# A gated cross-attention kernel: VectorE's softmax stage written as one list, with ScalarE's context copies and VectorE's Newton roots removed

## The chip, the cores and the metric

The kernel runs on one core of one Trainium2 chip. The metric is the device time of one execution in microseconds (us).

## What is computed

For each of 8 batches, `x` is 512 x 512 and the memory is 1601 x 256, all float32:

```python
memory_proj = einsum('bme,de->bmd', memory, W_mem)
scores = einsum('bnd,bmd->bnm', x, memory_proj) / sqrt(D)
attn = softmax(scores, axis=-1)
memory_context = einsum('bnm,bmd->bnd', attn, memory_proj)
gate = sigmoid(einsum('bnf,df->bnd', concatenate([x, memory_context], -1), W_gate) + b_gate)
fused = x + gate * memory_context
out = fused * rsqrt(mean(square(fused), -1) + 1e-6) * norm_w
```

## The kernel before, in words

The projection is never formed. The kernel multiplies x by `W_mem` (q, 256 columns), takes scores of q against the raw memory, sums the raw memory weighted by the exponentials (u), and only then multiplies u by `W_mem` (context) and by `V`, the product of `W_mem` and the second half of `W_gate` (gate). Each float32 factor is split into a rounded part (`_hi`, written by ScalarE) and the rest (`_lo`, written by VectorE, line 838), and each product takes three matmuls: hi by hi, hi by lo, lo by hi (lines 357 to 359, and 524 to 526 for the weighted sum).

The program is written by hand, one list for each engine, with semaphores between them. Each list has a repeat for b = 0, a hardware loop for b = 1 to 6, a repeat for b = 7 and a tail. One repeat has two stages.

**Scores stage.** TensorE computes 13 tiles of scores (the last of 65 rows). ScalarE copies each to `s` (`copy_s`), VectorE keeps a running maximum (L850) and splits the memory (`mem_lo`, pairs 0 to 5 of tiles here, by the table `SPLIT_BY_SCORES`).

**Softmax stage.** TensorE goes through this list: row sums of batch b - 1 (L459), its gate and context products for its four row tiles j, the x part of the gate of batch b for j = 0 to 3 (`gate_x`), then 13 tiles of the weighted sum, t = 0 to 12. Behind t = 9 stands the query product of batch b + 1 (`QUERY_AT = 9`). `gate_x` alternates between two PSUM banks, so from j = 2 it waits until VectorE's `add_bias` (L905) of j - 2 has emptied the bank; the query waits until VectorE's fourth `xt_lo` part, the rest of x transposed for batch b + 1, is written:

```python
pe.wait_ge(gx_done, NT * b + j - 1)
pe.wait_ge(xt_has_lo, DT * (b + 2))
```

Meanwhile, for each t, VectorE subtracts the column maximum (`shift`, L879), ScalarE takes the exponential (L673) and rounds it (L635), VectorE writes the rest (`p_lo_part`), and GpSimd adds the exponential to the row sums (`add_p`, L1155, 12 adds in a repeat). The epilogue of batch b - 1 is spread through VectorE's list by tables and conditions on t: `gate_input` (L934), `gate_ctx` (L984), `add_x` (L991); ScalarE does the `tanh`, scales the context out of PSUM by half the reciprocal row sum (`copy_ctx`, L696) and sums squares (L710). Then VectorE computes the reciprocal root by a bit trick and three Newton steps (`rms`, 11 small operations) and scales four tiles (`output`, L1020), which SyncE stores. The transposes of x and of the memory for batch b + 1 (L944, L960) stand in the same list.

In the tail, after b = 7, VectorE multiplies by `norm_w` ahead of the root (L1017) and ScalarE scales two of the four tiles (L831).

Of the kernel before, what the change touches and what calls it, by code (L numbers as in the profile page):

```python
# [30 lines left out]
ALU = mybir.AluOpType  # L31
# [6 lines left out]
P = 128  # L38
# [4 lines left out]
RSQRT_MAGIC = float(0x5F3759DF)  # L43
NEWTON_STEPS = 3


def xattn_kernel(nc: bass.Bass, x, mem, w, wg, b_gate, norm_w, out):
# [17 lines left out]
    with ExitStack() as ctx:  # L65
# [58 lines left out]
        nw_a = sb("nw_a", [P, NT])  # L124
        nw_b = sb("nw_b", [P, NT])
# [51 lines left out]
        ctx_copied, tanh_done, squares_done = sem("ctx_copied"), sem("tanh_done"), sem("squares_done")  # L177
# [7 lines left out]
        newton, out_done = sem("newton"), sem("out_done")  # L185

        normed, tail_done = sem("normed"), sem("tail_done")

        p_added = sem("p_added")

        NEWTON_OPS = 2 + 3 * NEWTON_STEPS
# [8 lines left out]
        X_AT = [6, 7, 9, 10]  # L200

        X_BLOCKS_AT = [4, 5, 7, 8]
        MEM_BLOCKS_AT = [10, 11]

# [30 lines left out]
        def _(sp):  # L235
# [103 lines left out]
            for j in range(NT):  # L339

                if 0 < j < NT - 1:
                    sp.wait_ge(tail_done, j)
                else:
                    sp.wait_ge(out_done, NT * (B - 1) + (1 if j == 0 else 2))
                sp.dma_start(out[B - 1, j * P : (j + 1) * P, :], fused[:, j, :]).then_inc(fused_free[j], 16)
# [6 lines left out]
        def _(pe):  # L352
# [280 lines left out]
        def _(act):  # L633
# [55 lines left out]
            def copy_ctx(b, j):  # L689

                act.wait_ge(pe_ctx, NT * b + j + 1)
                if j == 0:
                    act.wait_ge(r_done, b + 1)

                act.wait_ge(fused_free[j], 16 * (b + 1))
                nc.scalar.activation(fused[:, j, :], bank[CTX_BANK + j % 2][:, :], ACT.Copy,  # L696
                                     scale=r_half[:, j : j + 1]).then_inc(ctx_copied, 1)

# [51 lines left out]
            def iteration(b, first, last):  # L750
# [11 lines left out]
                if first:  # L762
                    for g in [*WG1T, V[0]]:
                        weights(g)
                    for t in range(MT + 1):
                        for q in SPLIT_BY_SOFTMAX.get(t, []):
                            mem_hi_part(b, q, first)
                        softmax(b, t, first)
                        if t == 1:
                            weights(V[1])  # L770
                        if not last and t - 1 in X_AT:
                            xt_hi_part(b + 1, X_AT.index(t - 1), False)
                        if not last and t == 12:
                            q_hi_part(b + 1, 0)
                            q_hi_part(b + 1, 1)
                else:
                    tanh(b - 1, 0)
                    copy_ctx(b - 1, 0)
                    tanh(b - 1, 1)
                    for t in range(MT + 1):  # L780
                        for q in SPLIT_BY_SOFTMAX.get(t, []):
                            mem_hi_part(b, q, first)
                        softmax(b, t, first)
                        if t in (0, 2, 3):
                            copy_ctx(b - 1, max(t, 1))
                        if t in (2, 3):
                            tanh(b - 1, t)
                        if t == 1:
                            squares(b - 1, 0)
                        if t - 2 in ADD_AT:  # L790
                            squares(b - 1, ADD_AT.index(t - 2) + 1)
                        if not last and t - 1 in X_AT:
                            xt_hi_part(b + 1, X_AT.index(t - 1), False)
                        if not last and t == 13:
                            q_hi_part(b + 1, 0)
                            q_hi_part(b + 1, 1)
# [23 lines left out]
            for j in range(NT):  # L820
                tanh(B - 1, j)
                copy_ctx(B - 1, j)
                if j >= 1:
                    squares(B - 1, j - 1)
            squares(B - 1, NT - 1)

            act.wait_ge(normed, NT - 1)

            act.wait_ge(newton, NEWTON_OPS * B)
            for j in range(1, NT - 1):  # L830
                nc.scalar.activation(fused[:, j, :], gate[:, j, :], ACT.Copy,  # L831
                                     scale=r_rms[:, j : j + 1]).then_inc(tail_done, 1)
# [3 lines left out]
        def _(dve):  # L836
# [54 lines left out]
            def softmax(b, t, with_x):  # L891

                if t + 3 < MT:
                    shift(b, t + 3)
                if with_x and t in X_AT:
                    xt_lo_part(b + 1, X_AT.index(t))
                p_lo_part(b, t)

# [38 lines left out]
            def transpose_x(b, k):  # L937

                if k >= 2:

                    dve.wait_ge(xt_has_lo, DT * b + k - 1)

# [4 lines left out]
            def transpose_mem(b, p):  # L947


                if p < 2:  # L950
                    dve.wait_ge(in_blocks[0], 16 * CT * BLOCKS * b)
                    if p == 1:
# [11 lines left out]
            def transpose_next(b, t, first):  # L964
                if t in X_BLOCKS_AT:
                    if t == X_BLOCKS_AT[0]:
                        if first:

                            dve.wait_ge(wt_split_lo, 8)
                        else:  # L970

                            dve.wait_ge(ctx_copied, NT * b)
                    transpose_x(b + 1, X_BLOCKS_AT.index(t))
                if t in MEM_BLOCKS_AT:
                    if t == MEM_BLOCKS_AT[0] and not first:

                        dve.wait_ge(z_done, NT * b)
                    transpose_mem(b + 1, MEM_BLOCKS_AT.index(t))
# [8 lines left out]
            def add_x(b, j):  # L987

                dve.wait_ge(gated, NT * b + j + 1)
# [4 lines left out]
            def rms(b):  # L994

                count = [NEWTON_OPS * b]

                def link(instruction):

                    count[0] = count[0] + 1  # L1000
                    instruction.then_inc(newton, 1)
                    dve.wait_ge(newton, count[0])


                dve.wait_ge(squares_done, NT * (b + 1))
# [186 lines left out]
```

## Time and profile before

| | |
|---|---|
| median of 3 runs | 561.4 us (561.13 to 561.5) |
| the profiled execution | 562.44 us, its span 560.6 us |
| busy: TensorE, VectorE | 541.7 us (97%), 503.4 us (90%) |
| busy: ScalarE, GpSimd | 336.2 us (60%), 134.1 us (24%) |
| one repeat, from one row sum to the next (b = 4) | 66.0 us |
| TensorE's mean granted clock | 0.99 |

Engines in the rows: PE is TensorE, PEld its weight loads, DVE VectorE, ACT ScalarE, POOL GpSimd. A duration in a row is longer than the engine's pitch: the next instruction starts before the last one's writes are seen. The pitch is read from the starts of neighbouring rows. Times of a timeline are counted from the start of the span.

### The profile page before, as it was taken

To read this page: it belongs to the slowest core of one execution; us is meant where nothing else is said; L and a number is where in the kernel's file an instruction comes from. 1 tells how busy PE (TensorE), PEld (TensorE's weight loads), DVE (VectorE), ACT (ScalarE), POOL (GpSimd) and SP (SyncE) were. 2 spreads that over 40 slices of the span, in tenths; PEclk is the share of its full clock that TensorE was granted. 3 is DMA by queue.
4 is the path that set the end of the run, shared out by engine and by line. 5 is a ranking of instruction groups with operands and counts; after the bars stand their busy time and mean duration, and the time that the engine had idled before them with its cause. 6 is when DMAs were issued, how large, how long until landed. Compare 5 with 4: busy or idle time off the path is not lost.

```text
span 560.6 us, 9004 instructions
## 1 busy us (share of the span) xinstructions
PE 541.7 (97%) x2432; PEld 438.8 (78%) x2432; DVE 503.4 (90%) x847; ACT 336.2 (60%) x633; POOL 134.1 (24%) x102
## 2 busy tenths in 40 slices
PE   8999999999999999999999999999999999999992
PEld 7777888878887788878888788887888778887871
DVE  4879959999899998899998998999988999889966
ACT  4676646665567646576366665666565864667534
POOL 0005600244003520055001440025300451005600
PEclk9999999999999999999999999999999999999988
DMA  9965371520683117711385115841088212100033
GB/s 226 260 127 83 90 132 50 98 73 18 148 176 97 37 50 136 167 68 37 98 163 104 56 37 134 171 114 40 0 170 177 75 37 99 52 23 20 0 114 112
DMA packets 184338, 54.25 MB, mean 97 GB/s; under 512 B 161528, under 2 KB 174848, under 8 KB 184320
## 3 DMA queue, kind: packets, MB, share of 16 engines
q1 hardware_dynamic: 183792, 53.52, 40.9%
q10 hardware_dynamic: 528, 0.52, 0.3%
q8 instruction: 8, 0.13, 0.1%
q14 instruction: 10, 0.08, 0.0%
HBM read 45.63 MB, written 8.39 MB: 96 GB/s over the span
## 4 chain that ended last, share of the span: by engine, by line
PE 66%; DVE 17%; issue 10%; SPq 3%; ACT 2%; DMA 2%; ACTq 0%; DVEq 0%
PE bank L357 14%; PE bank L358 13%; PE bank L359 13%; PE bank L524 7%; PE bank L525 7%; PE bank L526 7%; DVE p_lo L838 5%; DVE s L879 3%; DVE fused L984 2%; DVE fused L991 2%; DVE gate L905 2%; ACT fused L696 2%; DVE gate L934 2%; DMA fused<-in_L_xattn_W_gate_dram 2%; SPq L249 2%
## 5 line engine op out<-in xcount | busy, mean ns | idle before, releaser
L1155 POOL TENSOR_TENSOR psum_rows<-psum_rows,p_tmp 128x512 f32<-128x512 f32 (+1 forms) x88 | 122.5, 1392 | 85.4 <-ACT p_tmp L673 84.3
L838 DVE TENSOR_TENSOR p_lo<-p_tmp,p_hi 128x512 fp32r<-128x512 f32 (+1 forms) x104 | 92.3, 889 | 5.5 <-ACT p_hi L635 5.4
L673 ACT ACTIVATE p_tmp<-s 128x512 f32<-128x512 f32 (+1 forms) x104 | 65.2, 628 | 45.1 <-DVE s L879 44.5
L1155 POOL TENSOR_TENSOR psum_rows<-p_tmp 128x512 f32<-128x512 f32 x8 | 10.8, 1354 | 309.4 <-ACT p_tmp L673 309.4
L357 PE MATMUL bank<-q_hi,mt_hi 128*128 128x512 f32 (+1 forms) x208 | 81.7, 393 | 0.0
L358 PE MATMUL bank<-q_lo,mt_hi 128*128 128x512 f32 (+1 forms) x208 | 81.2, 390 | 0.0
L359 PE MATMUL bank<-q_hi,mt_lo 128*128 128x512 f32 (+1 forms) x208 | 81.1, 390 | 0.0
L525 PE MATMUL bank<-p_lo,mem_hi 128*128 128x512 f32 (+1 forms) x208 | 81.0, 389 | 0.0
L524 PE MATMUL bank<-p_hi,mem_hi 128*128 128x512 f32 (+1 forms) x208 | 81.0, 389 | 0.0
L526 PE MATMUL bank<-p_hi,mem_lo 128*128 128x512 f32 (+1 forms) x208 | 80.9, 389 | 0.0
L635 ACT ACTIVATE s<-bank 128x512 f32<-128x512 f32 (+1 forms) x104 | 62.0, 597 | 19.5 <-PE bank L359 19.1
L879 DVE TENSOR_TENSOR s<-s,bank 128x512 f32<-128x512 f32 (+1 forms) x104 | 68.5, 672 | 0.0
L850 DVE TENSOR_TENSOR run<-run,s 128x512 f32<-128x512 f32 (+1 forms) x88 | 59.9, 680 | 8.0 <-ACT s L635 5.6
L635 ACT ACTIVATE p_hi<-p_tmp 128x512 fp32r<-128x512 f32 (+1 forms) x104 | 63.5, 617 | 0.0
L357 PE MATMUL bank<-wg1t_hi,xt_hi 128*128 128x512 f32 x128 | 51.9, 405 | 5.9 <-DVE gate L905 5.9
L358 PE MATMUL bank<-wg1t_lo,xt_hi 128*128 128x512 f32 x128 | 49.9, 390 | 0.0
L359 PE MATMUL bank<-wg1t_hi,xt_lo 128*128 128x512 f32 x128 | 49.9, 390 | 0.0
L635 ACT ACTIVATE mt_hi<-bank 128x512 fp32r<-128x512 f32 (+1 forms) x56 | 30.2, 554 | 28.9 <-PE bank L359 28.9
L838 DVE TENSOR_TENSOR mt_lo<-bank,mt_hi 128x512 fp32r<-128x512 f32 (+1 forms) x56 | 34.5, 625 | 12.4 <-ACT mt_hi L635 12.4
L526 PEld LDWEIGHTS bank<-p_hi,mem_lo 128*128 128x128 f32 (+1 forms) x208 | 39.0, 188 | 8.2
L702 ACT ACTIVATE gate<-gate 128x512 f32<-128x512 f32 x32 | 20.2, 633 | 42.0 <-DVE gate L934 42.0
L524 PEld LDWEIGHTS bank<-p_hi,mem_hi 128*128 128x128 f32 (+1 forms) x208 | 39.0, 188 | 8.2
(93 smaller groups left out, 1057.6 us busy)
## 6 DMA issues: line engine op xcount, KB each, us to landing
mem_raw<-in_ctx_dram SPq DMA_DIRECT2D x48, 256.0 KB, 3.0
mem_blocks<-in_ctx_dram SPq DMA_DIRECT2D x64, 136.0 KB
x_again<-in_x_dram SPq DMA_DIRECT2D x32, 256.0 KB, 2.6
out_dram<-fused SPq DMA_DIRECT2D x32, 256.0 KB, 2.1
x_raw<-in_x_dram SPq DMA_DIRECT2D x112, 64.0 KB, 2.1
mem_blocks<-in_ctx_dram SPq DMA_DIRECT2D x56, 64.0 KB, 2.0
x_raw<-in_x_dram SPq DMA_DIRECT2D x4, 256.0 KB, 4.7
gate<-in_L_xattn_W_gate_dram SPq DMA_DIRECT2D x2, 512.0 KB, 6.1
```

The source lines that it names most:

```text
L357: nc.tensor.matmul(dst, a_hi, b_hi, start=(start and i == 0), stop=False)
L358: nc.tensor.matmul(dst, a_hi, b_lo, start=False, stop=False)
L359: last = nc.tensor.matmul(dst, a_lo, b_hi, start=False, stop=(stop and i == n - 1))
L524: nc.tensor.matmul(dst, mem_hi[0:r, t, cs], p_hi[0:r, t, :], start=(t == 0), stop=False)
L525: nc.tensor.matmul(dst, mem_hi[0:r, t, cs], p_lo[0:r, t % LO_RING, :], start=False, stop=False)
L526: last = nc.tensor.matmul(dst, mem_lo[0:r, t, cs], p_hi[0:r, t, :], start=False, stop=(t == MT - 1))
L635: return nc.scalar.activation(dst, src, ACT.Copy)
L673: nc.scalar.activation(p_tmp[0:r, t % TMP_RING, :], s[0:r, t, :], ACT.Exp, scale=float(D) ** -0.5).then_inc(exp_done, 1)
L838: return nc.vector.tensor_tensor(dst, src, hi.bitcast(F32), ALU.subtract)
L850: nc.vector.tensor_tensor(run[0:r, :], a, s[0:r, t, :], ALU.max).then_inc(run_done, 1)
L879: nc.vector.tensor_tensor(s[0:r, t, :], s[0:r, t, :], bank[MAX_BANK][0:r, :], ALU.subtract).then_inc(shifted, 1)
L1155: nc.gpsimd.tensor_tensor(psum_rows[0:r, :], a, p_tmp[0:r, t % TMP_RING, :], ALU.add).then_inc(p_added, 1)
```

## The change

1. `gate_ctx` reads the context from its accumulator bank in PSUM and no longer waits for a copy; ScalarE's `copy_ctx` is gone. The factor `r_half` moves into `add_x`, which becomes a scalar_tensor_tensor with a scalar per partition. TensorE's third and fourth context products now wait for `gated` in place of `ctx_copied`.
2. In the loop the root moves from VectorE to GpSimd: two small operations and a power with exponent -0.5, on 128 x 4 elements, behind its add for t = 9. VectorE's 11 Newton operations are gone; it waits for `rms_done` before the four outputs.
3. VectorE's softmax stage is one straight list, the same for all repeats but for the parts of the first and the last. Three of the epilogue's operations come earlier, the splits of memory pairs 4 and 5 move here from the scores stage, and the `xt_lo` parts stand behind `p_lo` of t = 8, 9, 10 and 11, in place of 5, 6, 8 and 9.
4. ScalarE's list follows: `tanh` behind t = 0, 2 (as 1, 2, 3 for j = 1, 2, 3), squares behind t = 3, 4, 5, 7, the hi parts of memory pairs 4 to 6 behind t = 6, 7, 8, the hi parts of x behind t = 9 to 12.
5. The tail computes the root in two parts, of tiles 0 to 2 and of tile 3: VectorE the mean, GpSimd the power, and VectorE all four outputs.

```diff
-        X_AT = [6, 7, 9, 10]
-        X_BLOCKS_AT = [4, 5, 7, 8]
-        MEM_BLOCKS_AT = [10, 11]
-        ADD_AT = [1, 3, 11]
-        SPLIT_BY_SCORES = {0: [0], 2: [1], 4: [2], 5: [3], 6: [4, 5]}
-        SPLIT_BY_SOFTMAX = {5: [6]}
+        SPLIT_BY_SCORES = {0: [0], 2: [1], 4: [2], 5: [3]}
+        SPLIT_BY_SOFTMAX = {6: 4, 7: 5, 8: 6}
+        TANH_AT, SQUARES_AT, NEXT_X_AT = {0: 1, 2: 2, 3: 3}, {3: 0, 4: 1, 5: 2, 7: 3}, {9: 0, 10: 1, 11: 2, 12: 3}
+        RMS_AT = 9
...
-                    pe.wait_ge(ctx_copied, NT * b + j - 1)
+                    pe.wait_ge(gated, NT * b + j - 1)
...
                 dve.wait_ge(tanh_done, NT * b + j + 1)
-                dve.wait_ge(ctx_copied, NT * b + j + 1)
-                nc.vector.scalar_tensor_tensor(fused[:, j, :], gate[:, j, :], 1.0, fused[:, j, :],
+                dve.wait_ge(pe_ctx, NT * b + j + 1)
+                dve.wait_ge(fused_free[j], 16 * (b + 1))
+                nc.vector.scalar_tensor_tensor(fused[:, j, :], gate[:, j, :], 1.0, bank[CTX_BANK + j % 2][:, :],
                                                ALU.add, ALU.mult).then_inc(gated, 1)
...
-                nc.vector.tensor_tensor(fused[:, j, :], fused[:, j, :], x_again[:, j % 2, :],
-                                        ALU.add).then_inc(fused_done, 1)
+                nc.vector.scalar_tensor_tensor(fused[:, j, :], fused[:, j, :], r_half[:, j : j + 1],
+                                               x_again[:, j % 2, :], ALU.mult, ALU.add).then_inc(fused_done, 1)
...
+                    gate_ctx(b - 1, 1)
+                    gate_input(b - 1, 2)
+                    add_x(b - 1, 1)
+                shift(b, 3)
+                p_lo_part(b, 0)
...
+                shift(b, 5)
+                p_lo_part(b, 2)
+                if not first:
+                    add_x(b - 1, 3)
+                add_bias(b, 0, first)
+                shift(b, 6)
+                p_lo_part(b, 3)
+                if not last:
+                    transpose_x(b + 1, 0, first)
+                shift(b, 7)
+                add_bias(b, 1, first)
...
+            def rms(b):
+
+                pool.wait_ge(squares_done, NT * (b + 1))
+                nc.gpsimd.tensor_tensor(mean_sq[:, :], sq_sum[:, :], one_in_d[:, :], ALU.mult).then_inc(mean_done, 1)
+                pool.wait_ge(mean_done, b + 1)
+                nc.gpsimd.tensor_tensor(mean_sq[:, :], mean_sq[:, :], eps_rows[:, :], ALU.add).then_inc(guarded, 1)
+                pool.wait_ge(guarded, b + 1)
+                nc.gpsimd.tensor_tensor(r_rms[:, :], mean_sq[:, :], minus_half[:, :], ALU.pow).then_inc(rms_done, 1)
...
+            gate_input(B - 1, 0)
             for j in range(NT):
+                gate_ctx(B - 1, j)
+                add_x(B - 1, j)
+                if j + 1 < NT:
+                    gate_input(B - 1, j + 1)
+                if j == NT - 2:
+                    tail_mean_sq(slice(0, NT - 1))
+
+            dve.wait_ge(rms_done, B)
+            output(B - 1, 0)
+            tail_mean_sq(slice(NT - 1, NT))
+            output(B - 1, 1)
+            output(B - 1, 2)
+
+            dve.wait_ge(rms_done, B + 1)
+            output(B - 1, 3)
```

Where the list moves VectorE's work, first place: the hardware loop, up to the first `add_bias` (gate<-bank,bias_rows), for which TensorE's third `gate_x` waits. Before:

```order
L934 SCALAR_TENSOR_TENSOR gate<-bank,r_sum,gate 128x512
L991 TENSOR_TENSOR fused<-fused,x_again 128x512
L879 TENSOR_TENSOR s<-s,bank 128x512
L838 TENSOR_TENSOR p_lo<-p_tmp,p_hi 128x512
...
L934 SCALAR_TENSOR_TENSOR gate<-bank,r_sum,gate 128x512
L984 SCALAR_TENSOR_TENSOR fused<-gate,fused 128x512
L879 TENSOR_TENSOR s<-s,bank 128x512
L838 TENSOR_TENSOR p_lo<-p_tmp,p_hi 128x512
...
L905 TENSOR_TENSOR gate<-bank,bias_rows 128x512
```

and in the change:

```order
L923 SCALAR_TENSOR_TENSOR fused<-gate,bank 128x512
...
L878 SCALAR_TENSOR_TENSOR gate<-bank,r_sum,gate 128x512
...
L933 SCALAR_TENSOR_TENSOR fused<-fused,r_half,x_again 128x512
L831 TENSOR_TENSOR s<-s,bank 128x512
L790 TENSOR_TENSOR p_lo<-p_tmp,p_hi 128x512
L923 SCALAR_TENSOR_TENSOR fused<-gate,bank 128x512
L831 TENSOR_TENSOR s<-s,bank 128x512
L790 TENSOR_TENSOR p_lo<-p_tmp,p_hi 128x512
L933 SCALAR_TENSOR_TENSOR fused<-fused,r_half,x_again 128x512
...
L849 TENSOR_TENSOR gate<-bank,bias_rows 128x512
```

The additions of x for tiles 2 and 3 (fused<-fused,r_half,x_again) and the gate product of tile 3 (fused<-gate,bank) now stand ahead of this `add_bias`, where three of them stood behind it.

Second place: the same loop, up to the fourth `xt_lo`, for which TensorE's query product waits. Before:

```order
L838 TENSOR_TENSOR p_lo<-p_tmp,p_hi 128x512
L944 STREAM_TRANSPOSE bank<-x_raw 128x512
L879 TENSOR_TENSOR s<-s,bank 65x512
...
L838 TENSOR_TENSOR xt_lo<-bank,xt_hi 128x512
L838 TENSOR_TENSOR p_lo<-p_tmp,p_hi 128x512
...
L838 TENSOR_TENSOR xt_lo<-bank,xt_hi 128x512
L838 TENSOR_TENSOR p_lo<-p_tmp,p_hi 128x512
...
L960 STREAM_TRANSPOSE bank<-mem_blocks 128x512
L991 TENSOR_TENSOR fused<-fused,x_again 128x512
L838 TENSOR_TENSOR p_lo<-p_tmp,p_hi 128x512
L960 STREAM_TRANSPOSE bank<-mem_blocks 128x512
L838 TENSOR_TENSOR p_lo<-p_tmp,p_hi 65x512
```

and in the change:

```order
L790 TENSOR_TENSOR p_lo<-p_tmp,p_hi 128x512
L790 TENSOR_TENSOR mem_lo<-mem_raw,mem_hi 65x256
...
L790 TENSOR_TENSOR xt_lo<-bank,xt_hi 128x512
L894 STREAM_TRANSPOSE bank<-x_raw 128x512
L790 TENSOR_TENSOR p_lo<-p_tmp,p_hi 128x512
...
L790 TENSOR_TENSOR xt_lo<-bank,xt_hi 128x512
...
L914 STREAM_TRANSPOSE bank<-mem_blocks 128x512
L790 TENSOR_TENSOR p_lo<-p_tmp,p_hi 128x512
...
L790 TENSOR_TENSOR xt_lo<-bank,xt_hi 128x512
L914 STREAM_TRANSPOSE bank<-mem_blocks 128x512
L790 TENSOR_TENSOR p_lo<-p_tmp,p_hi 65x512
```

The fourth `xt_lo` stood ahead of `p_lo` of t = 10 and of both transposes of the memory; now `p_lo` of t = 10 and 11 and the first of these transposes stand ahead of it.

## Rows read from the trace of the kernel before

**Rows 1.** Page, part 1: busy us (share of span) and instructions of each engine.

```profile
PE 541.7 (97%) x2432; PEld 438.8 (78%) x2432; DVE 503.4 (90%) x847; ACT 336.2 (60%) x633; POOL 134.1 (24%) x102
```

**Rows 2.** Waits, all engines: engine, line waited for: us in total, times, longest us.

```profile
PEld bank L357 <- DVE gate L905: 11.9, 14, 1.1
...
DVE fused L984 <- ACT fused L696: 7.1, 14, 0.8
```

**Rows 3.** Timeline of PE, repeat b = 4: start us, us, engine, line, op, names, shapes, count.

```profile
295.50 0.95 PE L459 MATMUL bank<-ones,psum_rows 128*128 128x1 f32 x8
...
313.44 0.39 PE L359 MATMUL bank<-wg1t_hi,xt_lo 128*128 128x512 f32 x1
...
314.02 0.50 PE L357 MATMUL bank<-wg1t_hi,xt_hi 128*128 128x512 f32 x1 [0.19 <-DVE gate L905]
...
316.65 0.39 PE L359 MATMUL bank<-wg1t_hi,xt_lo 128*128 128x512 f32 x1
...
317.73 0.50 PE L357 MATMUL bank<-wg1t_hi,xt_hi 128*128 128x512 f32 x1 [0.69 <-DVE gate L905]
...
334.18 0.39 PE L357 MATMUL bank<-xt_hi,w_hi 128*128 128x512 f32 x1
...
361.50 0.95 PE L459 MATMUL bank<-ones,psum_rows 128*128 128x1 f32 x8
```

**Rows 4.** Timeline of DVE, repeat b = 4, around the waits.

```profile
298.55 0.75 DVE L934 SCALAR_TENSOR_TENSOR gate<-bank,r_sum,gate 128x512 f32<-128x512 f32 x1
...
301.28 0.74 DVE L934 SCALAR_TENSOR_TENSOR gate<-bank,r_sum,gate 128x512 f32<-128x512 f32 x1
...
302.54 1.88 DVE L879 TENSOR_TENSOR s<-s,bank 128x512 f32<-128x512 f32 x3
...
313.29 0.68 DVE L905 TENSOR_TENSOR gate<-bank,bias_rows 128x512 f32<-128x512 f32 x1
...
331.95 0.67 DVE L838 TENSOR_TENSOR xt_lo<-bank,xt_hi 128x512 fp32r<-128x512 f32 x1
```

**Rows 5.** Timeline of DVE and POOL, repeat b = 4: work that shares SBUF reads.

```profile
305.87 1.19 DVE L838 TENSOR_TENSOR p_lo<-p_tmp,p_hi 128x512 fp32r<-128x512 f32 x1
...
309.29 1.62 DVE L838 TENSOR_TENSOR p_lo<-p_tmp,p_hi 128x512 fp32r<-128x512 f32 x1
...
317.60 1.15 DVE L984 SCALAR_TENSOR_TENSOR fused<-gate,fused 128x512 f32<-128x512 f32 x1
...
305.15 1.36 POOL L1155 TENSOR_TENSOR psum_rows<-p_tmp 128x512 f32<-128x512 f32 x1 [37.97 <-ACT p_tmp L673]
```

**Rows 6.** Timeline of DVE, end of the stage: the roots and the four outputs.

```profile
336.67 0.14 DVE L1006 TENSOR_SCALAR mean_sq<-sq_sum 128x4 f32<-128x4 f32 x1
...
338.82 2.74 DVE L1020 SCALAR_TENSOR_TENSOR fused<-fused,r_rms,norm_rows 128x512 f32<-128x512 f32 x4
```

**Rows 7.** Timeline of ACT and POOL, repeat b = 4: an exponential and the add it feeds.

```profile
306.10 0.62 ACT L673 ACTIVATE p_tmp<-s 128x512 f32<-128x512 f32 x1
...
306.89 1.33 POOL L1155 TENSOR_TENSOR psum_rows<-psum_rows,p_tmp 128x512 f32<-128x512 f32 x1 [0.38 <-ACT p_tmp L673]
```

**Rows 8.** Groups by line: us busy, mean ns of one | idle before, releaser.

```profile
L1155 POOL TENSOR_TENSOR psum_rows<-psum_rows,p_tmp 128x512 f32<-128x512 f32 (+1 forms) x88 | 122.5, 1392 | 85.4 <-ACT p_tmp L673 84.3
...
L1180 POOL MEMSET const-float32-1.0<- 128x1 f32 x1 | 0.1, 99 | 0.0
```

**Rows 9.** Timeline of PE and DVE, first repeat, b = 0.

```profile
49.36 0.67 DVE L905 TENSOR_TENSOR gate<-bank,bias_rows 128x512 f32<-128x512 f32 x1
...
70.12 0.39 PE L357 MATMUL bank<-xt_hi,w_hi 128*128 128x512 f32 x1
```

**Rows 10.** Timeline of DVE, tail after the last repeat.

```profile
539.77 0.75 DVE L934 SCALAR_TENSOR_TENSOR gate<-bank,r_sum,gate 128x512 f32<-128x512 f32 x1 [1.41 <-PE bank L359]
...
555.95 0.75 DVE L1020 SCALAR_TENSOR_TENSOR fused<-fused,r_rms,norm_rows 128x512 f32<-128x512 f32 x1
```

**Rows 11.** Page, part 6: DMA issues, KB each, median us to landing.

```profile
out_dram<-fused SPq DMA_DIRECT2D x32, 256.0 KB, 2.1
```

More of the change, by code:

```diff
@@ L339, in _ @@
             for j in range(NT):
[L341 to L345, printed above, removed]
+                store(B - 1, j)
             for j in range(NT):
@@ L687, in softmax @@
                     p_hi_part(b, t - 1)
[L689 to L697, printed above, removed]
             def tanh(b, j):
@@ L764, in iteration @@
                         weights(g)
[L765 to L775, printed above, removed]
                 else:
                     tanh(b - 1, 0)
[L778 to L796, printed above, removed]
+                for t in range(MT + 1):
+                    softmax(b, t, first)
+                    if first and t == 1:
+                        weights(V[1])
+                    if not first and t in TANH_AT:
+                        tanh(b - 1, TANH_AT[t])
+                    if not first and t in SQUARES_AT:
+                        squares(b - 1, SQUARES_AT[t])
+                    if t in SPLIT_BY_SOFTMAX:
+                        mem_hi_part(b, SPLIT_BY_SOFTMAX[t], first)
+                    if not last and t in NEXT_X_AT:
+                        xt_hi_part(b + 1, NEXT_X_AT[t], False)
+                if not last:
+                    q_hi_part(b + 1, 0)
+                    q_hi_part(b + 1, 1)
                 if not last:
@@ L821, in _ @@
                 tanh(B - 1, j)
[L822 to L832, printed above, removed]
+                squares(B - 1, j)
         @block.vector
@@ L962, in transpose_mem @@
                     mem_blocks[:, :, r0:r1, :]).then_inc(mt_done, 1)
[L964 to L978, printed above, removed]
@@ L1055, in iteration @@
                     shift(b, 2)
-                    for t in range(MT):
-                        for q in SPLIT_BY_SOFTMAX.get(t, []):
-                            mem_lo_part(b, q)
-                        softmax(b, t, not last)
-                        if t == 1:
-                            weights(V[1])
-                        if 1 <= t < 1 + NT:
-                            add_bias(b, t - 1, first)
-                        transpose_next(b, t, first)
                 else:
@@ L1090, in iteration @@
-                    rms(b - 1)
+                    gate_ctx(b - 1, 1)
[3 more added lines that the diff above has]
+                p_lo_part(b, 0)
+                if first:
+                    weights(V[1])
+                else:
+                    gate_ctx(b - 1, 2)
+                    gate_input(b - 1, 3)
+                    add_x(b - 1, 2)
+                shift(b, 4)
+                p_lo_part(b, 1)
+                if not first:
+                    gate_ctx(b - 1, 3)
@@ new lines, in iteration @@
+                p_lo_part(b, 5)
+                add_bias(b, 2, first)
+                shift(b, 9)
+                p_lo_part(b, 6)
+                mem_lo_part(b, 4)
+                shift(b, 10)
+                add_bias(b, 3, first)
+                p_lo_part(b, 7)
+                mem_lo_part(b, 5)
+                shift(b, 11)
+                p_lo_part(b, 8)
+                if not last:
+                    xt_lo_part(b + 1, 0)
+                    transpose_x(b + 1, 2, first)
+                shift(b, 12)
@@ new lines, in iteration @@
+                p_lo_part(b, 9)
+                mem_lo_part(b, 6)
+                if not last:
+                    xt_lo_part(b + 1, 1)
+                    transpose_x(b + 1, 3, first)
+                p_lo_part(b, 10)
+                if not last:
+                    xt_lo_part(b + 1, 2)
+                    transpose_mem(b + 1, 0, first)
+                p_lo_part(b, 11)
+                if not last:
+                    xt_lo_part(b + 1, 3)
+                    transpose_mem(b + 1, 1, first)
@@ L1091, in iteration @@
+                p_lo_part(b, 12)
+                if not first:
+                    dve.wait_ge(rms_done, b)
                     for j in range(NT):
```

98 lines of the change are left out of this document (38 added, 60 removed).

## Prediction

> **What bounds the kernel now.** I read the page's busy shares first, then the waits, then the timeline of one repeat in the loop. TensorE is busy for 541.7 us of the 560.6 [rows 1], so at most 19 us of gaps can be won, and every new gap on it is paid in full. Its waits inside the repeats have one name: `add_bias`, whose 14 waits come before the third and fourth `gate_x` [rows 2]. In repeat b = 4 the second `gate_x` issues its last matmul at 313.44, the next could follow 0.23 us later at 313.67 and starts at 314.02 (0.35 late); the fourth could start at 316.88 and starts at 317.73 (0.85 late) [rows 3]. So a repeat of 66.0 us has 1.2 us of waiting. The query product at 334.18 follows without a wait. VectorE is what TensorE waits for: from 301.28 on it works through its list with hardly a break, and its first `add_bias` starts at 313.29 [rows 4]. Each place of that list therefore has a due time: the two `add_bias` are late already, and the fourth `xt_lo`, from 331.95 to 332.62, is 1.5 us early for the query [rows 3, 4].
>
> **Prices.** VectorE's pitch for 128 x 512 is 0.595 us (three `shift` with a last duration of 0.68 take 1.88 [rows 4]) and 0.66 with a scalar per partition (four outputs take 2.74 [rows 6]). A consumer on another engine starts about 0.78 us after the start of its producer: an exponential starts at 306.10, its add on GpSimd at 306.89 [rows 7]. VectorE's operations with two SBUF inputs do not run beside a GpSimd add: the `p_lo` at 305.87 takes 1.19 in place of 0.68 because an add started at 305.15, so the add keeps it out for 1.2 us from its start; others lose up to 0.9 [rows 5]. The Trainium skill (SBUF — State Buffer, Who interferes with whom) gives this as a rule: such an operation and a GpSimd one that reads SBUF exclude each other for the whole instruction, and one SBUF input is free of it. The trace agrees. By that rule the new gate product, with its context from PSUM, cannot be held up, as the old one was at 317.60 (1.15).
>
> **Part by part, one repeat of the loop.** I walk the four lists with these prices, from the row sums at 295.50. (The old lists, walked so, give the third and fourth `gate_x` within 0.1 us of their rows and a repeat of 65.8, so I trust it to some tenths.)
>
> *The copies go.* VectorE's waits for them are 7.1 us in 14 times, 0.5 each [rows 2]. Little of it comes back: the second `gate_input` waits for TensorE's product and starts at 301.15 in place of 301.28; the additions of x cost 0.065 more each with their scalar. The first `shift` starts at 302.4, against 302.54. On ScalarE four copies of 0.6 go, but it is busy 60% [rows 1] and waits for VectorE: nothing.
>
> *Up to the first `add_bias`.* It stands behind 19 full operations now, behind 22 in the change: +1.8. The second gate product comes 0.25 earlier, three adds with a scalar cost 0.2 more, and the waits behind adds fall from 1.9 to about 1.5 (the addition of x and two `p_lo` meet one each). It starts at about 314.5 in place of 313.29, and the third `gate_x` at 315.2, 1.2 later. The second `add_bias` then has four operations ahead of it where it had three with two long waits: it starts at 317.5, and the fourth `gate_x` at 318.2 against 317.73. **Cost 0.5.**
>
> *Up to the fourth `xt_lo`.* Six more operations stand ahead of it than before: the last addition of x, memory pairs 4 and 5, `p_lo` of t = 10 and 11, and one memory transpose: 3.65 us. Waits behind adds fall from 4.0 to 3.5, two transposes wait 0.13 each for their own `xt_lo`, and 0.3 us comes from above. It starts at 335.1 in place of 331.95, so the query can start at 335.8, against 334.18. By the late `gate_x` TensorE would be there at 334.7: a new wait of about 1.1. **Cost 1.65 for both together,** six times (b = 1 to 6): 9.9.
>
> *Moved work that is covered.* The splits of pairs 4 and 5 leave the end of the scores stage, 1.2 us of VectorE's time; the first `gate_input` then waits for TensorE's product in place of VectorE, and the second does so anyway (above), so nothing comes of it. Newton's 2.1 us, from 336.67 to 338.82 [rows 6], lie behind `p_lo` of t = 12 and ahead of splits that wait for TensorE's query: nothing.
>
> *GpSimd's root.* Three more operations stand among its adds; adds 10 to 12 queue behind them, and VectorE's `p_lo` and the last memory split behind those. No row shows a power. The bounds are the 0.10 us of a memset and the 1.39 us of a full add [rows 8]; the two plain ones on 4 columns I put near the memset, 0.15 each. For the power I take 0.5: few columns, but long arithmetic for each. That is in the 1.65. At 0.1 the repeat costs about 1.2, at 1.4 about 2.5; a power may also be longer than an add. [...]
>
> *b = 0.* The first `add_bias`, at 49.36, slips behind another `shift` and `p_lo`, and from it to the query the same list follows. I take the query at 71.9 in place of 70.12 [rows 9]: +1.8, bounds 0.9 and 3.
>
> *b = 7.* No query; 0.5 at the fourth `gate_x`, and 0.3 back as the outputs no longer hold up the last split of u: +0.2.
>
> *Tail.* Each tile becomes a ring of `gate_input`, tanh, gate product, addition: 0.65 + 0.14 + 0.6 + 0.7 + 0.7 or some 2.9 us, where TensorE's 12 matmuls gave 2.7. From 539.77 on the last addition ends at about 552.4; the last output follows the third at 554.8, against 555.95 [rows 10]. The stores leave one by one, the last alone: 2.1 us to land [rows 11], where four at once took until the end of the span. Gain 1.7, bounds 1.0 and 2.2.
>
> **Sum.** 1.8 + 9.9 + 0.2 - 1.7 = +10.2. On the profiled execution's 562.4 that is 572.6; the median of the runs is 1.0 below it, so 571.6 us. With all bounds low (0.9 + 7.2 - 2.2) it is 567, with all high (3 + 15 + 0.5 - 1) 579. A measurement of this kernel can tell 0.2% (1.1 us) from no change.
>
> **Rivals.**
> *A lost race for the port, b = 1 to 7.* In my walk the last addition of x asks at 313.83 and the add of t = 4 is ready at 313.85: a tie. If GpSimd wins, the addition waits 1.2 us, the first `add_bias` with it, and the phase of all later ones changes; I price it at 1.2 to 2.4 more a repeat: 571.6 + 8.4 to 16.8, likeliest 585. For it: 0.9 us waits are in the rows [rows 5]. Against: half of the ways to cut it fall the other way. Chance 0.27.
> *A long power* (2 us or more): each us beyond 0.5 costs about a us in six repeats, and some in the tail: 580 to 600. Chance 0.09.
> *Faster, by the port.* If the new order lets VectorE's two-input operations fall between the adds, its 4.0 us of waits go: the first `add_bias` is then in time (314.5 - 1.5 = 313.0), the fourth `xt_lo` too, and all of 1.2 us times 7 and the tail are won: 561.4 - 8.4 - 1.7 = 551. It decides from 2.0 us less waiting on. Against it: `exp` and `p_hi` of neighbouring tiles feed both engines at the same moment. Chance 0.07, some of it in part.
> *No change:* losses cut to the tail's gain; it needs the fourth `xt_lo` before 334.1. Chance 0.04.
>
> **How the numbers follow.** The forecast has 0.53, its own range being 567 to 579. The range of 565 to 588 leaves out the faster case and no change (0.11) and the longest powers. Slower: 0.53 + 0.27 + 0.09 = 0.89.
>
> **What would show it.** Right: repeats of about 67.7 us; a new wait of TensorE at L344 for `xt_lo`, near 1 us, seven times; the third `gate_x` over 1 us late, the fourth hardly; no wait for a context copy; the last output about 1 us nearer to the last addition. Wrong: a query without a wait, or a first `add_bias` within 17.8 us of the row sums.

## The result, and the profile after

The changed kernel takes 579.95 us (median of 4 runs, 579.86 to 580.35), the kernel before 561.45 beside it: ratio 1.0327, 95% interval [1.0312, 1.0342]. It is slower, 18.5 us in all, inside the range of 565 to 588 but 8.4 above the forecast of 571.6. The two profiled spans, 577.8 and 560.6, divide so (the marks are PE rows: first `gate_x`, query, row sums):

| stretch | before, us | after, us | difference | forecast |
|---|---|---|---|---|
| start to the first `gate_x` of b = 0 | 45.19 | 46.42 | +1.2 | 0 |
| from there to the query of b = 0 | 24.93 | 30.85 | +5.9 | +1.8 |
| six repeats, row sums of b = 1 to those of b = 7 | 396.1 | 409.7 | +13.6 | +9.9 |
| b = 7, to its own row sums at the end | 42.6 | 43.9 | +1.3 | +0.2 |
| the tail, from there to the end | 24.4 | 19.6 | -4.8 | -1.7 |

(From the query of b = 0 to the row sums of b = 1 both take 27.3.) The first line is not the change: in the profiles of the kernels below the same stretch lies between 44.5 and 47.3. The spans differ by 17.2 and the medians by 18.5, mostly because the profiled execution of the kernel before lies 1.0 above its median.

Page of the changed kernel, part 1, beside [rows 1]:

```profile
PE 542.7 (94%) x2432; PEld 437.5 (76%) x2432; DVE 485.7 (84%) x760; ACT 313.6 (54%) x599; POOL 165.3 (29%) x128
```

VectorE has 17.7 us less work and TensorE the same; TensorE idles more. The waits of the changed kernel, beside [rows 2] (us in total, times, longest):

```profile
PEld bank L344 <- DVE gate L849: 26.6, 15, 4.4
...
PE bank L344 <- DVE xt_lo L790: 2.9, 6, 0.5
...
DVE bank L894 <- DMA x_raw<-in_x_dram: 3.9, 1, 3.9
```

The copies are gone from the list, as meant, but TensorE waits for `add_bias` (L849) over twice as long, and now for the last `xt_lo` too, in six repeats, and VectorE once for a load. One repeat, TensorE's timeline at b = 4, beside [rows 3] (L446 are the row sums, xt_hi,w_hi is the query):

```profile
309.42 0.95 PE L446 MATMUL bank<-ones,psum_rows 128*128 128x1 f32 x8
...
327.39 0.39 PE L346 MATMUL bank<-wg1t_hi,xt_lo 128*128 128x512 f32 x1
...
330.15 0.50 PE L344 MATMUL bank<-wg1t_hi,xt_hi 128*128 128x512 f32 x1 [2.37 <-DVE gate L849]
...
333.15 0.50 PE L344 MATMUL bank<-wg1t_hi,xt_hi 128*128 128x512 f32 x1
...
350.27 0.49 PE L344 MATMUL bank<-xt_hi,w_hi 128*128 128x512 f32 x1 [0.48 <-DVE xt_lo L790]
...
377.71 0.28 PE L446 MATMUL bank<-ones,psum_rows 128*128 128x1 f32 x2
```

The third `gate_x` stands 20.73 us behind the row sums (18.52 before) and could have followed 0.23 after 327.39, at 327.62: 2.53 late. The fourth is only 0.1 late, the query 0.6 (349.63 possible). The repeat is 68.29. Why the third is so late, VectorE's and GpSimd's timelines at that place:

```profile
326.78 1.03 DVE L790 TENSOR_TENSOR p_lo<-p_tmp,p_hi 128x512 fp32r<-128x512 f32 x1
327.73 1.77 DVE L933 SCALAR_TENSOR_TENSOR fused<-fused,r_half,x_again 128x512 f32<-128x512 f32 x1
329.42 0.68 DVE L849 TENSOR_TENSOR gate<-bank,bias_rows 128x512 f32<-128x512 f32 x1
```

```profile
327.68 1.26 POOL L1118 TENSOR_TENSOR psum_rows<-psum_rows,p_tmp 128x512 f32<-128x512 f32 x1 [0.43 <-ACT p_tmp L660]
```

The last addition of x (L933) comes 0.05 us after GpSimd's fifth add, which is that of t = 5 (the prediction, and the expectation of the run with `add_bias` first, call it t = 4), and takes 1.77 in place of 0.74: the race of the first rival, lost, and so in all seven repeats (1.76 to 1.84). By the Trainium skill (SBUF — State Buffer, Who interferes with whom) two such operations shut each other out; the row agrees. VectorE's list up to the query ends with

```profile
344.30 1.51 DVE L790 TENSOR_TENSOR mem_lo<-mem_raw,mem_hi 65x256 fp32r<-65x256 f32 x1
...
349.47 0.67 DVE L790 TENSOR_TENSOR xt_lo<-bank,xt_hi 128x512 fp32r<-128x512 f32 x1
```

That is a split of a quarter of the size that takes 1.51 in place of 0.40 (its row in b = 0), held up by GpSimd's adds behind the root, and the fourth `xt_lo` 40.05 after the row sums (36.45 before, [rows 3, 4]). In b = 0 VectorE and then TensorE show what the forecast missed altogether:

```profile
57.49 0.73 DVE L894 STREAM_TRANSPOSE bank<-x_raw 128x512 f32<-128x512 f32 x1 [3.92 <-DMA x_raw<-in_x_dram]
58.13 0.67 DVE L831 TENSOR_TENSOR s<-s,bank 128x512 f32<-128x512 f32 x1
58.72 0.67 DVE L849 TENSOR_TENSOR gate<-bank,bias_rows 128x512 f32<-128x512 f32 x1
```

```profile
59.44 0.80 PE L344 MATMUL bank<-wg1t_hi,xt_hi 128*128 128x512 f32 x1 [3.99 <-DVE gate L849]
60.03 0.63 PE L345 MATMUL bank<-wg1t_lo,xt_hi 128*128 128x512 f32 x1
60.46 0.63 PE L346 MATMUL bank<-wg1t_hi,xt_lo 128*128 128x512 f32 x1
60.88 0.63 PE L344 MATMUL bank<-wg1t_hi,xt_hi 128*128 128x512 f32 x1
```

The first transpose of the next x now stands ahead of the second `add_bias`, and the last of its data lands at 57.4. TensorE idles 4.2 us, and after that its matmuls follow at 0.43 us in place of 0.23 up to 62.16: the granted clock is 0.50 from 59.44 to 62.44, so 1.2 GHz, another 1.3 us.

### The profile page after: what moved, and what is told of

It is laid out like the page before. It is cut to its first block, busy times and chain, and to the rows that moved or that the text cites. A ratio compares the mean times of both kernels' runs of the same rounds, so it can differ in the third digit from the quotient of the medians.

```text
span 577.8 us, 8830 instructions
## 1 busy us (share of the span) xinstructions
PE 542.7 (94%) x2432; PEld 437.5 (76%) x2432; DVE 485.7 (84%) x760; ACT 313.6 (54%) x599; POOL 165.3 (29%) x128
## 4 chain that ended last, share of the span: by engine, by line
PE 75%; DVE 13%; issue 4%; SPq 4%; DMA 2%; ACT 1%; DVEq 0%; ACTq 0%
PE bank L344 17%; PE bank L346 16%; PE bank L345 16%; PE bank L511 8%; PE bank L512 8%; PE bank L513 8%; DVE fused L933 5%; DVE p_lo L790 3%; DVE fused L923 2%; DMA fused<-in_L_xattn_W_gate_dram 2%; SPq L241 2%; SPq L233 1%; PE bank L531 1%; PE bank L446 1%; DVE gate L849 1%
## 5 line engine op out<-in xcount | busy, mean ns | idle before, releaser
L1118 POOL TENSOR_TENSOR psum_rows<-psum_rows,p_tmp 128x512 f32<-128x512 f32 (+1 forms) x88 | 136.7, 1553 | 63.0 <-ACT p_tmp L660 60.8
L790 DVE TENSOR_TENSOR p_lo<-p_tmp,p_hi 128x512 fp32r<-128x512 f32 (+1 forms) x104 | 80.2, 772 | 0.0
L622 ACT ACTIVATE s<-bank 128x512 f32<-128x512 f32 (+1 forms) x104 | 62.0, 596 | 19.6 <-PE bank L346 19.2
L344 PEld LDWEIGHTS bank<-wg1t_hi,xt_hi 128*128 128x128 f32 x128 | 24.4, 191 | 31.5 <-DVE gate L849 26.6
L512 PEld LDWEIGHTS bank<-p_lo,mem_hi 128*128 128x128 f32 (+1 forms) x208 | 39.1, 188 | 8.1
```

The source lines that it names most:

```text
L344: nc.tensor.matmul(dst, a_hi, b_hi, start=(start and i == 0), stop=False)
L512: nc.tensor.matmul(dst, mem_hi[0:r, t, cs], p_lo[0:r, t % LO_RING, :], start=False, stop=False)
L622: return nc.scalar.activation(dst, src, ACT.Copy)
L790: return nc.vector.tensor_tensor(dst, src, hi.bitcast(F32), ALU.subtract)
L1118: nc.gpsimd.tensor_tensor(psum_rows[0:r, :], a, p_tmp[0:r, t % TMP_RING, :], ALU.add).then_inc(p_added, 1)
```

## What costs: the list or the other parts

My theory after this: the straight list alone costs, by its order; rival theories put part of it on the other edits. So each of them was put alone into the old kernel, and then all of them with the old list. Ratios here and below are to the kernel before, run on the same chip.

**Context from the accumulator alone.** The gate product, the addition with its scalar and ScalarE's list as in the change's diff (without `copy_ctx`), VectorE's old list:

```diff
-                        if t in (0, 2, 3):
-                            copy_ctx(b - 1, max(t, 1))
```

> The old softmax list, Newton root and tail; only ScalarE's copies of the context go, VectorE's gate product reads the accumulator and the addition of x carries the scalar 1/(2 sum). Theory A (the list alone is what costs, the other parts are neutral or small gains): repeats of the loop within 65.3 and 66.0 us, VectorE's waits for a copy gone, the whole between 557 and 561.4 us. Theory B (the new gate products cost too: a scalar on each addition, reads of the accumulator in VectorE's busy stretch): repeats of 66.2 to 66.6 us, the whole 563 to 566.

Measured: 556.4 us, ratio 0.9889 [0.9846, 0.9932]; repeats of 65.3. TensorE waits 6.4 us for `add_bias` in 7 times, where it was 11.9 in 14. Theory A, the whole 0.6 below its range; in its profile the tail is 2 us shorter as well (22.5), which is the clock (below). The forecast gave nothing for this edit inside the loop; in the old list it gives 0.7 a repeat.

**Root by GpSimd alone**, behind its last add:

```diff
+                    if t == 12:
+                        rms(b - 1)
...
-                    rms(b - 1)
+                    dve.wait_ge(rms_done, b)
```

> The old list, copies and tail; in the loop the root is GpSimd's three operations after its add of t = 12, and VectorE's eleven small operations go. Theory A: the Newton steps lay behind VectorE's last p_lo and ahead of splits that wait for TensorE anyway, and behind the last add GpSimd holds nobody up: 561.4 within 1 us, repeats of 66.0. Theory B (three GpSimd operations of 2.3 us together cost where they stand): the outputs start later than before, the split of the query with them, repeats of 66.5 or more, the whole 565 or more.

Measured: 560.86, ratio 0.9982 [0.9958, 1.0006], repeats of 66.0: neutral, theory A.

**The new tail alone**, with `gate_input` of the next tile still ahead of the gate product:

```diff
+            gate_ctx(B - 1, NT - 1)
+            tail_mean_sq(slice(0, NT - 1))
+            add_x(B - 1, NT - 1)
+            dve.wait_ge(rms_done, 1)
+            output(B - 1, 0)
```

> The old loop with its Newton roots and copies; only the end is new: the roots in two parts by GpSimd's power, all four outputs on VectorE, four stores one by one, while gate_input of the next tile stays ahead of the gate product of this one. Theory A (the tail's gain is its two-part root and the separate stores): 2 to 4 us less than before, 557.5 to 559.5. Theory B (the gain of 4.3 us came from VectorE's new order at the end, or from TensorE's clock not falling there): within 1 us of 561.4, with the clock of the last stretch below full as before.

Measured: 560.35, ratio 0.9972 [0.9953, 0.9991]: the tail takes 22.6 us in its profile against 24.4. Between the theories: the two-part root and the separate stores give 1.8 (the forecast had 1.7 for the whole tail). Most of what the changed kernel won besides is told by TensorE's clock at the start of the tail, in windows of 7 us from the last row sums on: the kernel before, then the run with the root alone, whose tail is written the same.

```profile
536.17:543.17 7.00, 6.60 (x27) 5.35 (x26) 2.90 (x7) 2.02 (x4) 0.00 (x0) 0.76 0.59 205
```

```profile
535.65:542.65 7.00, 7.00 (x36) 5.85 (x35) 4.10 (x9) 2.88 (x6) 0.00 (x0) 1.00 0.52 169
```

(busy us and count of PE, PEld, DVE, ACT, POOL; granted clock; DMA share; GB/s.) At 0.76 it issues 27 matmuls where it issues 36 at 1.00, and the tails take 24.4 and 22.35 us. The clock falls so in the profiles of the kernel before, of the new tail alone and of the last run below (`ADD_AT` alone), and in these three TensorE idled 0.4 us for a split of u just ahead of the fall; in the others, the changed kernel too (1.00), it did neither. So 2 of the 4.8 us between the two profiled tails are the clock. That the idling makes the clock fall is not shown by a run of its own.

**All parts, old list.**

> All of the change but the straight list: context from the accumulator, root by GpSimd's power after its add of t = 12, the new tail with gate_input of the next tile ahead. Theory A (the list costs all of the loss, and hides gains of the rest): 554 to 558.5 us, loop repeats of 65.3 to 66.0, the tail some 3 to 4 us shorter than before. Theory B (the parts cost too): above 562.

Measured: 554.12, ratio 0.9851 [0.981, 0.9892]; repeats of 65.3, the tail 20.6. The rest of the change is worth 7.5 us, and the list, 579.95 against 554.12, costs 26 (VectorE's list with ScalarE's that follows it and the order in the tail; some 1.4 of it stand ahead of the first `gate_x`, in the stretch that is not the change). Theory A is shown.

## Where in the list

**The load in b = 0.** Only in the first repeat, the first two transposes of x behind the third `add_bias`:

```diff
                 add_bias(b, 2, first)
+                if first:
+                    transpose_x(b + 1, 0, first)
+                    transpose_x(b + 1, 1, first)
```

> The changed kernel, where in the first repeat alone VectorE's first two transposes of the next x stand behind the third add_bias, and so ahead of no add_bias of t = 0 to 2. Theory A (the 3.92 us in which VectorE waits for the load of x stand ahead of the second add_bias, and TensorE's fourth gate product waits with it): 3.3 to 4.2 us less, 575.8 to 576.6, row sums of b = 1 at 100.5 to 101.3 in place of 104.58. Theory B (the load is late for all that follows too, and the transposes' place only moves the wait to the query): within 1 us of 579.95.

Measured: 575.37, ratio 1.025 [1.0233, 1.0268], so 4.6 less. Theory A. From the first `gate_x` to the query it is 26.3 us (30.85, and 24.93 before): 4.5 come back, wait and clock, and the 1.4 that stay are the list, near the 1.8 forecast. Most of them are a wait at the query (TensorE's timeline):

```profile
70.86 0.50 PE L344 MATMUL bank<-xt_hi,w_hi 128*128 128x512 f32 x1 [0.98 <-DVE xt_lo L790]
```

The row sums of b = 1 at 98.35 owe 1.9 more to an earlier start of the first `gate_x`. b = 1 and 2 then take 68.8 and 68.6 in place of 68.3: over the 4 us from their third `gate_x` on the granted clock is 0.57 and 0.62, in the other repeats 1.00.

**The lost race.** The first `add_bias` ahead of the last addition of x:

```diff
+                add_bias(b, 0, first)
                 if not first:
                     add_x(b - 1, 3)
-                add_bias(b, 0, first)
```

> The changed kernel with the first add_bias ahead of the last addition of x, which in the profile lost the port to GpSimd's add of t = 4 by 0.05 us and took 1.77 in place of 0.75. Theory A (the lost race is what makes the third gate product 1.0 us later than forecast): the third gate product starts 17.9 to 18.8 us after the row sums in place of 20.73, and each repeat gains 1.0 to 2.3 us. Theory B (VectorE has too much in its list ahead of the query, whatever stands first): the third gate product comes 1.7 us earlier, but the wait comes back at the fourth or at the query, and the repeat stays within 0.6 us of 68.28.

Measured: 575.32, ratio 1.0239 [1.0216, 1.0261]. The third `gate_x` comes 1.7 us earlier (19.02 behind the row sums), the repeat gets 0.6 shorter (67.68): the waits move, TensorE's timeline of b = 4, whose row sums stand at 307.57:

```profile
326.59 0.50 PE L344 MATMUL bank<-wg1t_hi,xt_hi 128*128 128x512 f32 x1 [0.69 <-DVE gate L849]
...
330.69 0.50 PE L344 MATMUL bank<-wg1t_hi,xt_hi 128*128 128x512 f32 x1 [1.05 <-DVE gate L849]
...
347.81 0.49 PE L344 MATMUL bank<-xt_hi,w_hi 128*128 128x512 f32 x1 [0.51 <-DVE xt_lo L790]
```

Mostly theory B. The addition still waits for the same add, 0.4 us now, and the 0.6 us that VectorE saves there arrive at the query undiminished.

**The last addition of x behind the fourth `xt_lo`**, where the old list had it (root and squares of that tile moved behind it):

```diff
                     xt_lo_part(b + 1, 3)
                     transpose_mem(b + 1, 1, first)
+                if not first:
+                    add_x(b - 1, 3)
```

> The changed kernel with the last addition of x behind the fourth xt_lo and the second memory transpose, its squares behind the last p_hi, and the root behind the add of t = 12 (which alone changed nothing). Theory A (as before: VectorE's list up to the fourth xt_lo): 0.66 us of the addition and the 1.1 us it waited for the port go, the third gate product starts 1.5 us earlier and the query too: repeats of 66.4 to 67.2 us. Theory B (the third gate product was all that was wrong, and with it early the waits end): the first add_bias in time, no wait left ahead of the third gate product, repeats near the 65.3 of the old list with the other parts.

Measured: 567.73, ratio 1.0098 [1.0071, 1.0125], repeats of 66.6. Theory A: 1.7 a repeat, which is the addition's 0.66 and the 1.1 that it waited. TensorE still waits 0.67 ahead of the third `gate_x` and 0.50 ahead of the query.

**The root's place.**

```diff
-        RMS_AT = 9
+        RMS_AT = 12
```

> The changed kernel with the root of the loop behind GpSimd's last add (t = 12) in place of behind the one of t = 9. Theory A (the three GpSimd operations, 2.3 us together, push adds 10 to 12, and these push VectorE's p_lo and xt_lo ahead of the query): the query starts about 1.5 to 2 us earlier in each repeat, repeats of 66.8 to 67.3 us where the changed kernel has 68.28, the whole 568 to 573. Theory B (the lost 2.28 us come from the late additions of the bias alone): repeats of 68.0 to 68.3, the whole 578 to 580.

Measured: 579.25, ratio 1.0314 [1.0296, 1.0333], repeats of 68.3, as theory B has it: theory A falls, the root costs nothing where it stands, though it takes 2.4 us. GpSimd and VectorE of the changed kernel at b = 4:

```profile
339.38 0.73 POOL L1123 TENSOR_TENSOR mean_sq<-sq_sum,one_in_d 128x4 f32<-128x4 f32 x1
340.19 0.53 POOL L1125 TENSOR_TENSOR mean_sq<-mean_sq,eps_rows 128x4 f32<-128x4 f32 x1
340.79 1.02 POOL L1127 TENSOR_TENSOR r_rms<-mean_sq,minus_half 128x4 f32<-128x4 f32 x1
```

```profile
339.97 0.68 DVE L790 TENSOR_TENSOR mem_lo<-mem_raw,mem_hi 128x512 fp32r<-128x512 f32 x1
```

and with the root behind t = 12 (GpSimd, VectorE), 0.29 us earlier on the clock of the trace:

```profile
339.45 1.45 POOL L1118 TENSOR_TENSOR psum_rows<-psum_rows,p_tmp 128x512 f32<-128x512 f32 x1 [0.35 <-ACT p_tmp L660]
...
346.74 0.20 POOL L1123 TENSOR_TENSOR mean_sq<-sq_sum,one_in_d 128x4 f32<-128x4 f32 x1
```

```profile
339.67 1.78 DVE L790 TENSOR_TENSOR mem_lo<-mem_raw,mem_hi 128x512 fp32r<-128x512 f32 x1
```

While the small operations run, no add holds VectorE up; without them the same split waits 1.1 us at once, as the later, smaller one did in the changed kernel. The wait changes its place, hardly its size.

**The query one step later, and two memory splits back in the scores stage.** Two ways to take the query's wait away:

```diff
-        QUERY_AT = 9
+        QUERY_AT = 10
```

> The changed kernel with TensorE's query product behind the weighted product of t = 10 in place of t = 9. Theory A (VectorE is late as a whole): TensorE's wait for xt_lo (0.48 in a repeat) goes but the later weighted products wait for p_lo instead, repeats of 67.7 to 68.1 us. Theory B (TensorE's place for the query is what costs): the same wait goes and nothing takes its place, and the one ahead of the third gate product stays: 68.28 - 0.5 = 67.8 a repeat; a gain over 0.7 a repeat would speak against both.

```diff
-        SPLIT_BY_SCORES = {0: [0], 2: [1], 4: [2], 5: [3]}
-        SPLIT_BY_SOFTMAX = {6: 4, 7: 5, 8: 6}
+        SPLIT_BY_SCORES = {0: [0], 2: [1], 4: [2], 5: [3], 6: [4, 5]}
+        SPLIT_BY_SOFTMAX = {8: 6}
```

> The changed kernel with the splits of memory pairs 4 and 5, on ScalarE and VectorE, back at the end of the scores stage; all else of the straight list stays. Theory A (a repeat lasts as long as VectorE's list up to the fourth xt_lo, and each operation ahead of it is paid whether or not an add_bias is late): two operations of 0.6 us and part of the waits for the port around them go, the query starts 1.2 to 2.0 us earlier, repeats of 66.3 to 67.1 us in place of 68.28. Theory B (the repeat is set by the late third gate product, whose 2.4 us of idle time shift all that follows): 68.0 to 68.3.

Measured: 579.61, ratio 1.0316 [1.0294, 1.0338], and 579.03, ratio 1.0291 [1.0262, 1.032]. Neither gains clearly. In both profiles two of the six repeats take 67.5 us, and the query's wait is gone from all six; the other four take 68.6 to 68.8. These four differ from the two by the clock after the wait for the third `gate_x`. Windows of 4 us around it, the run with the later query, in a short repeat and in a long one:

```profile
399.49:403.50 4.01, 3.29 (x13) 2.47 (x14) 4.01 (x8) 2.50 (x5) 1.33 (x2) 1.00 0.00 0
```

```profile
330.88:334.88 4.00, 3.32 (x8) 2.65 (x9) 4.00 (x8) 2.52 (x5) 1.35 (x2) 0.57 0.00 0
```

The wait is 2.4 us both times; 13 matmuls follow, or 8. So the wait at the query held 0.8 us a repeat, and what the clock takes in four of six repeats takes it back. (With the splits back it falls in b = 7 too, which lasts 45.6 in place of 43.9.) Neither run's theory A is shown: no wait for `p_lo` takes the place of the query's, and with the splits back 1.2 to 2.0 was expected and 0.8 is all there is, since the late third `gate_x` sets a repeat of 67.5. Nor is a theory B as it stands: with the splits back the mean repeat of 68.3 is in its range, but by the clock, which it didn't have; and with the later query 0.8 is over the 0.7 that was to speak against both. Why the clock falls in some repeats of these two kernels and of the one with the later transposes, and in none of the changed kernel's profile, with the same wait ahead of the third `gate_x`, stays open.

## A version that beats both

The old list with the new parts had one wait of TensorE left in a repeat, at the fourth `gate_x`, with an addition of x ahead of the `add_bias` that it waits for. One line of numbers moves that addition behind the second `add_bias`; the tail takes the changed kernel's order as well, which the cut does not show:

```diff
-        ADD_AT = [1, 3, 11]
+        ADD_AT = [1, 4, 11]
```

> All of the change but the straight list, as in the run of the old list, and besides: the second late addition of x one step later in the old list (t = 4 in place of 3, behind the second add_bias), and the changed kernel's own order in the tail. Theory A (with the late addition out of its way the first and second add_bias come before TensorE needs their banks, and nothing else is late): TensorE's last waits in the loop go, repeats of 64.4 to 64.9 us in place of 65.34, the tail 0.5 to 1 us shorter, the whole 547 to 550. Theory B (the addition then waits for GpSimd's add where it now stands, and the wait moves to a later add_bias or to the query): repeats of 65.2 or more, the whole 553 or more.

Measured: **549.03 us, ratio 0.9767 [0.9746, 0.9788]**: 12.5 less than before, 30.9 less than the changed kernel. Repeats of 64.5, and TensorE has no wait for `add_bias` at all. The tail takes 20.3, so nearly all of the gain on the run with the old list (554.12) is the moved addition. TensorE's busy share in the page:

```profile
PE 535.5 (98%) x2432; PEld 438.4 (80%) x2432; DVE 479.5 (87%) x760; ACT 315.4 (58%) x599; POOL 151.8 (28%) x128
```

At b = 4 VectorE's two first `add_bias` start 17.1 and 19.1 us after the row sums at 293.14 (VectorE's timeline; the first of them started 17.8 behind in the kernel before, [rows 3, 4], and 20.0 in the changed one):

```profile
310.23 0.68 DVE L884 TENSOR_TENSOR gate<-bank,bias_rows 128x512 f32<-128x512 f32 x1
...
312.25 0.68 DVE L884 TENSOR_TENSOR gate<-bank,bias_rows 128x512 f32<-128x512 f32 x1
```

How much of that needs the change's parts? The kernel before, with nothing but this:

```diff
-        ADD_AT = [1, 3, 11]
+        ADD_AT = [2, 4, 11]
```

> The kernel before with one line of numbers changed: the second and the third addition of x one step later in VectorE's list (t = 2 and 4 in place of 1 and 3), so that each stands behind an add_bias or a gate_input that it stood ahead of; copies, Newton root and tail as before. Theory A (TensorE's waits for add_bias come from the additions ahead of them, and the rest of the old list has room): repeats of 64.6 to 65.2 us in place of 66.0, the whole 553.5 to 556.5, most of what the best version gains in its loop without any of the change's parts. Theory B (the copies of the context keep VectorE too late for that, and only without them the order helps): repeats of 65.7 or more, 559 or more.

Measured: 554.37, ratio 0.9861 [0.9835, 0.9888], repeats of 64.9: theory A. Two additions moved by a step win as much as context, root and tail together (0.9861 and 0.9851).

## Why the prediction was right in sign and 8 us short

- *The sum.* The median is 8.4 above the forecast. By the table 7.0 of this are 1.2 at the start, 4.1 in b = 0, 3.7 in the loop and 1.1 in b = 7, less 3.1 in the tail; 1.0 is that the profiled execution of the kernel before stood so far above its median. 579.95 is also the low end of the first rival (571.6 + 8.4), and that is luck: its race was lost, but at half of its lowest price, and b = 0, which no rival had, filled the gap. That the tail took 3.1 back, 2 of them by the clock, is luck too.
- *Due times.* The mechanism held: TensorE waits at the same places, and the third `gate_x` is over 1 us late, the fourth hardly, the query waits (0.6 in six repeats; the prediction had near 1 in seven, but in b = 0 there is none). With 64.5 as a repeat without waits (the best version's), 2.53 + 0.15 + 0.65 give 67.9 of the 68.3. Another 0.3 is that each first matmul after a wait holds the next one back by 0.1 (330.15, then 330.49 in place of 330.38); some 0.1 stays unassigned.
- *Up to the first `add_bias`.* Forecast 19.0 us behind the row sums (314.5), measured 20.0. The 1.0 is the lost race, which stood among the rivals with 0.27; it was a tie in my walk, which could not tell, and a loss in every repeat.
- *The race's price* was mis-sized, 1.2 to 2.4 a repeat. The repeat is 68.28 where the walk without it said 67.65: 0.6, and the run with `add_bias` ahead of the addition gives just 0.6 back. (That run does not take the race away: the addition still waits 0.4.)
- *Up to the fourth `xt_lo`.* Forecast 335.1 - 295.5 = 39.6, measured 40.05; the query at 40.85 against 40.3. The step stands, though its terms as written (3.65 - 0.5 + 0.26 + 0.3) add up to 3.7 and it counts 3.15; the wait there was 0.6, not 1.1, because the third `gate_x` was later.
- *GpSimd's root.* 2.4 us where I took 0.8, and no cost at all. The power alone took 1.02, and the bound "at 1.4 the repeat costs about 2.5" failed with it: the walk put the adds' delay on VectorE, and left out that VectorE runs free of them meanwhile.
- *The copies.* Nothing in the sum, and 0.7 a repeat in the old list. In the new list it is part of the walk and can't be read apart.
- *b = 0* was the term that failed, +1.8 with bounds of 0.9 and 3, measured +5.9. I moved a transpose ahead of an `add_bias` in my walk and looked at its engines, not at its load: 3.9 us of waiting, and 1.3 of clock. The trace of before would have told it: SyncE issues the sixteenth load of this x at 53.9 and they land 1.9 to 2.7 us after their issue, so the data are there at about 56, while the transpose, two operations behind an `add_bias` that I had at about 50.5, was due near 52 (an estimate from [rows 9] and the prediction's shift).
- *b = 7:* +0.2 forecast, +1.3 measured: it loses the race as the others do (1.84), and its fourth `gate_x` comes 1.4 later than before, where I had 0.5.
- *Tail:* the ring is 2.83 us a tile (forecast 2.9, though its terms add up to 2.8). The forecast's 1.7 for the whole is near the 1.8 of the run with the new tail alone; the clock gave another 2 that no step had. The last 1.0 (the old-list run has 20.6, the changed kernel 19.6) is 0.4 up to the last addition and 0.6 behind it; in the best version, with the same order, it is 0.3, so no more than that is shown to be the order's.

## What to carry to other kernels

When a static list is the bottleneck's feeder, write down for each product the moment by which its consumer needs it, and move what nobody is waiting for (here an addition of x) behind it; two numbers changed by one were worth 8 us (554.37 against 562.27 beside it), a rewrite of the whole list cost 26. An operation moved to the front takes its inputs' arrival times with it, and in the first round of a pipeline the load can be what is late, and the trace before the change says when it lands. A short idle stretch of TensorE may cost more than its length: read the granted clock behind it.

## What the runs showed of the hardware that I had not expected

- GpSimd's power takes 1.02 us on 128 x 4, and 0.99 on 128 x 1 in the tail; its small multiplication 0.20 alone and 0.73 beside a VectorE operation with two SBUF inputs. The Trainium skill (GPSIMD Engine Reference, Elementwise — side-by-side cycle accounting) puts VectorE's dispatch of an instruction at 156 ns and gives GpSimd two software hops for it where VectorE has one, without a time. VectorE's small root operations on 128 x 4 took 0.16 to 0.17 in the kernel before; what of GpSimd's 0.20 and 1.02 is dispatch no run here breaks down.
- VectorE's operations with two SBUF inputs are not held by GpSimd's 4-column ones in a way that shows (a `p_lo` that starts at 341.17, inside the power of 340.79 to 341.81, takes 0.68), but by a full add of 1.26 to 1.45 for 1.0 to 1.1 of it (1.77 and 1.78 for 0.74 and 0.68).
- In the profiles TensorE's granted clock fell to its lower level after 0.4 us of idling in the tail of three kernels, after 2.4 us in four of six repeats of two others and in two of six of a third, and not at all after the same 2.4 us in the six repeats of the changed kernel and of the run with the root behind t = 12. Each fall in a repeat cost 1.1 to 1.3 us.
